# Sums, scores and a turn take other places in the inner order of a rotary attention stage

## The chip, the cores and the metric

The kernel runs on one core of one Trainium2 chip. The metric is the device time of one execution in microseconds (us). The core has TensorE (PE in the profile, its weight loads PEld), VectorE (DVE), ScalarE (ACT), GpSimd (POOL) and SyncE (SP), each with its own list of instructions that it works off in order. They meet at semaphores: an instruction may wait until a counter has a value, and may count one up when it is done.

## The reference, cut to what matters

Two layers act on x of 2 x 2048 tokens x 512. The change lies in the first, a cross attention with 128 keys per batch, 16 heads of 64, rotated queries and keys, capped scores and a causal mask:

```
q = layer_norm(query, g, b); k = layer_norm(ctx, g, b); v = layer_norm(ctx, g, b)
qh, kh = rope(heads(q @ Wq)), rope(heads(k @ Wk)); vh = heads(v @ Wv)
aw = 30 * tanh(einsum('nhtd,nhTd->nhtT', qh, kh) / sqrt(64) / 30)
p = softmax(where(pad | causal, -inf, aw))
x = x + einsum('nhtT,nhTd->nhtd', p, vh).merged @ Wo
```

Behind it come a feed-forward layer in quantised numbers, a second cross attention and a layer of eight experts. The change doesn't touch them.

## The kernel before

The first stage works in 16 chunks of 256 tokens, and a body numbered n = 0 to 16 overlaps two of them: it finishes the attention of chunk n, adds the output of chunk n-1 to x (O0 and O1, one for each 128 tokens), and prepares the queries of chunk n+1. Bodies 1 to 6 and 9 to 12 are loops on the chip, the others are written out. In each chunk the 16 heads are four units of four heads (numbers 0 to 3). For each unit:

- `project`: 48 matmuls for two units (three products of high and low parts), into a bank named Q0 to Q3; DVE rotates the result (`rotate_begin`, `rotate_end`) into `q`.
- `scores(n, b, p)`: q times keys, with 64 rows of the array for each head; ACT takes tanh and then exp (`exponentials`). On the chunks with n = 0 and n = 8 DVE multiplies a causal mask in between (`mask`).
- `sums(p)`: a matmul with 32 columns for each head adds up the probabilities over the keys; `values(n, b, p)`: probabilities times values, 64 columns for each head; ACT copies the result (`raw`).
- When all four sums are in, DVE takes their reciprocal, PE spreads it over the heads (`spread`, banks B0 to B3) and DVE multiplies (`weigh`); ACT and POOL make high and low parts of it.
- `output(t)`: 24 matmuls of 512 columns; DVE adds the bank to x (`add_out`).
- `turn_x` (X0 and X1): four transposes each of the next chunk's normalised rows; ACT scales them (`x_turned`), casts them to high parts (`x_high`), POOL makes the low parts (`x_low`), which the next projection needs.

Only two banks serve all of Q, O, X and B, in a ring whose order is Q2, Q3, O0, X0, X1, O1, Q0, Q1, B0 to B3; `begin` waits until the bank's last user has let it go. Scores have two buffers of their own, and so have the probabilities: `exponentials` of unit p waits for sums and values of unit p-2. `sums(p)` and `values(p)` wait for the exponentials of p (on masked chunks for the mask). The order of the work is written out by hand for each engine. In the code the flag `first` marks body 0, which had an order of its own.

Of the kernel before, what the change touches and what calls it, by code (L numbers as in the profile page):

```python
# [268 lines left out]
def rope_attention_stage(nc, io, xres, front_offset, ident, seen, ahead):  # L269
# [8 lines left out]
    with ExitStack() as stage:  # L278
        def sb(name, shape, dt=F32):
            return stage.enter_context(nc.sbuf_tensor("a_" + name, shape, dt))  # L280
# [58 lines left out]
        raw = xres[:, LAST_X:LAST_X + 4, 0:D]  # L339
# [78 lines left out]
        def turn_x(out, k, rows):  # L418
            for i in range(2):
                at = slice((2 * k + i) * P, (2 * k + i + 1) * P)  # L420
                for t in range(NT):
                    last = nc.tensor.transpose(out[:, i, t * P:(t + 1) * P], rows[:, t, at], ident[:])  # L422
            last.then_inc(bank_full, 1)
# [185 lines left out]
        xn = sb("xn", [P, NT, D])  # L609
# [23 lines left out]
        def of_spread(x, g):  # L633

            return x[:, g // 2, :, g % 2, :]

        with nc.Block() as block:
# [83 lines left out]
            @block.scalar  # L721
            def _(act):
                def x_turned(n, k, full, src):
                    act.wait_ge(bank_full, full)
                    for i in range(2):
                        m = 2 * k + i
                        last = nc.scalar.activation(x_full[:, m, :], src[:, i, :], ACT.Identity, bias=shift[:, m:m + 1], scale=gain[:, m:m + 1])  # L727
                    last.then_inc(freed["act"], 1)

                def x_high(k, emptied):  # L730
                    act.wait_ge(freed["act"], emptied)
                    at = slice(2 * k, 2 * k + 2)
                    nc.scalar.copy(x_hi[:, at, :], x_full[:, at, :]).then_inc(x_hi_ready, 1)  # L733

                def exponentials(n, b, p):
                    unit = n * UNITS + p
                    buf = probs[:, p % 2]
                    act.wait_ge(score_full, unit + 1)
                    if p >= 2 or not isinstance(n, int) or n >= 1:
                        act.wait_ge(pv_full, unit - 1)  # L740
                        act.wait_ge(summed, unit - 1)
                    nc.scalar.activation(buf, score_ps[:, p % 2], ACT.Tanh, scale=1.0 / (DH0 ** 0.5 * GROK)).then_inc(capped, 1)  # L742
                    act.wait_ge(capped, unit + 1)
                    nc.scalar.activation(buf, buf, ACT.Exp, bias=pad_bias[:, b:b + 1], scale=GROK).then_inc(exped, 1)

                exponentials(0, 0, 0)

                def body(n, c, b, b_next):
                    s = plan(n)

                    def use(what):
                        return ring.use(n, 0, s[what])

                    def raw(p):
                        act.wait_ge(pv_full, n * UNITS + p + 1)
                        if p % 2 == 0 and (not isinstance(n, int) or n >= 1):
                            act.wait_ge(attn_lo_ready, UNITS * (n - 1) + p + 2)
                        nc.scalar.copy(attn[:, p // 2, p % 2], pv_ps[:]).then_inc(raw_ready, 1)  # L758

                    def attn_high(g):  # L760
                        act.wait_ge(freed["dve"], use(f"B{g}").emptied[1])
                        nc.scalar.copy(of_spread(attn_hi, g), of_spread(attn, g)).then_inc(attn_hi_ready, 1)  # L762

                    first = isinstance(n, int) and n == 0
                    if "Q2" in s:
                        exponentials(n, b, 1)
                        raw(0)
                    if first:
                        exponentials(n, b, 2)
                    if "X0" in s:  # L770
                        x_turned(n + 1, 0, use("X0").full, use("X0").out)
                    if "Q2" in s and not first:
                        exponentials(n, b, 2)
                    if "Q2" in s and not first:
                        raw(1)
                        exponentials(n, b, 3)
                    if "X0" in s:
                        x_turned(n + 1, 1, use("X1").full, use("X1").out)
                        x_high(0, use("X0").emptied[1])
                        x_high(1, use("X1").emptied[1])  # L780
                    if first:
                        raw(1)
                        exponentials(n, b, 3)
                    if "Q2" in s:
                        raw(2)
                    if "X0" in s:
                        exponentials(n + 1, b_next, 0)
                    if "Q2" in s:
                        raw(3)
                        for g in range(4):  # L790
                            attn_high(g)

                chunks(act, body)
                act.wait_ge(ahead.ld_clip, 16)
                nc.scalar.activation(ahead.sigm[:], ahead.clip[:], ACT.Exp, scale=-1.0).then_inc(ahead.sig_exp, 1)
                for g in range(len(ahead.GROUPS)):
                    if g == ahead.GROUPS_AHEAD:
                        nc.scalar.activation(warm[:], minus_half[:, 0:1], ACT.Silu)
                    act.wait_ge(ahead.turned, g + 1)
                    ahead.take(nc, g, turn_places[g % len(turn_places)]).then_inc(ahead.taken, 1)  # L800
# [224 lines left out]
            def _(pe):  # L1025
# [10 lines left out]
                def place(h):  # L1036

                    return h % 2 * 2 + h // 2
# [3 lines left out]
                def scores(n, b, p):  # L1042
                    unit = n * UNITS + p
                    pe.wait_ge(q_ready, unit + 1)
                    if p >= 2 or not isinstance(n, int) or n >= 1:
                        pe.wait_ge(capped, unit - 1)
                    for h in range(4):
                        rows, m = slice(h % 2 * DH0, (h % 2 + 1) * DH0), 2 * p + h // 2
                        last = nc.tensor.matmul(score_ps[:, p % 2, place(h), :], keysT[rows, m, b * KEYS:(b + 1) * KEYS], q[rows, p % 2, h // 2, :],  # L1049
                                                start=True, stop=True)  # L1050
                    last.then_inc(score_full, 1)
# [23 lines left out]
                def body(n, c, b, b_next):  # L1075
                    s = plan(n)

                    def begin(what):
                        u = ring.use(n, 0, s[what])
                        who, count = u.reuse  # L1080
                        pe.wait_ge(freed[who], count)
                        return u.out

                    def sums(p):
                        probabilities(n, b, p)
                        if p == 0 and (not isinstance(n, int) or n >= 1):
                            pe.wait_ge(recip_ready, n)
                        for h in range(4):
                            last = nc.tensor.matmul(sum_ps[32 * h:32 * (h + 1), 0, :], sum_to[:, UNITS - 1 - p:UNITS - 1 - p + 32], probs[:, p % 2, place(h), :],
                                                    start=(p == 0), stop=(p == UNITS - 1))  # L1090
                        last.then_inc(summed, 1)
# [48 lines left out]
                    first = isinstance(n, int) and n == 0  # L1140
# [13 lines left out]
                    if "X0" in s:  # L1154
                        pe.wait_ge(xn_ready, 1 + NT * (n + 2))
                        turn_x(begin("X0"), 0, xn)
                    if first:
                        turn_x(begin("X1"), 1, xn)
                        sums(1)
                        scores(n, b, 3)  # L1160
                    elif "Q2" in s:
                        sums(0)
                        sums(1)
                        scores(n, b, 2)
                        scores(n, b, 3)
                    if "Q2" in s:
                        values(n, b, 1)
                    if first:
                        sums(2)
                    if "X0" in s and not first:  # L1170
                        turn_x(begin("X1"), 1, xn)
                    if "O0" in s:
                        output(1)
                    if "Q2" in s and not first:
                        sums(2)
                    if "Q2" in s:
                        sums(3)
                    if "X0" in s:
# [1750 lines left out]
```

## Time and profile before

| | before |
|---|---|
| three runs, us | 1512.35, 1513.0, 1513.22 |
| profiled execution, us | 1513.22 |
| its span, first to last instruction, us | 1511.4 |
| mean granted TensorE clock | 0.986 |
| PE, PEld busy, us | 1442.1, 1076.8 |
| DVE, ACT, POOL busy, us | 1183.9, 878.7, 501.7 |

The span is that of the one execution that the profiler took; its time has 1.8 us around the span. The first stage ends at some 622 us of it. In the rows a matmul's line tells what it is: L422 a turn, L430 the projection, L1032 to L1034 the output, L1049 scores, L1064 values, L1089 sums, L1103 spread. On ACT, L727 is `x_turned`, L742 tanh, L744 exp, L758 `raw`. One matmul in the code can be two instructions of the trace (f32 operands), so that the sums of one unit are eight.

### The profile page before, as it was taken

The numbers are of one execution on the slowest core, as the hardware profiler recorded it, in microseconds if no ns is written. First come the engines' busy times: TensorE is split into PE (matmuls) and PEld (weight loads), VectorE is DVE, ScalarE is ACT, GpSimd is POOL, SyncE is SP. The second block draws the span as 40 slices with busy tenths as digits, with TensorE's granted clock in tenths as the row PEclk, the third lists the DMA queues.
The fourth block names the chain that finished last, engine by engine and source line by source line (L and its number), as shares of the span: only waits on it lengthen the run. The fifth ranks groups of instructions, "written<-read, shape, count | busy, mean of one in ns | idle before, by whom it ended". The sixth has DMA issues, their size and how long they took to land. (4 is left out here: it accounts for less than half of the span.)

```text
span 1511.4 us, 30065 instructions
## 1 busy us (share of the span) xinstructions
PE 1442.1 (95%) x10610; PEld 1076.8 (71%) x10634; DVE 1183.9 (78%) x2421; ACT 878.7 (58%) x2090; POOL 501.7 (33%) x442
## 2 busy tenths in 40 slices
PE   7899999999999999899998998999999999998996
PEld 5677777777777777644443467888888877776885
DVE  6678788887887666788878967888888896786875
ACT  2444444444444443765558747888888876763442
POOL 0122222222222221200004644555555654664333
PEclk9999999999999999999999999999999999999998
DMA  8411111110111101133107610000000024225641
GB/s 300 177 46 45 45 45 45 46 41 15 37 36 45 36 8 77 46 153 154 77 1 282 240 41 3 3 2 2 4 3 3 3 86 174 114 102 180 208 148 58
DMA packets 47807, 118.34 MB, mean 78 GB/s; under 512 B 9422, under 2 KB 15950, under 8 KB 46032
## 3 DMA queue, kind: packets, MB, share of 16 engines
q1 hardware_dynamic: 42016, 100.03, 19.0%
q0 software_dynamic: 5680, 16.85, 2.8%
q8 instruction: 67, 1.10, 0.3%
q14 instruction: 44, 0.36, 0.1%
HBM read 78.90 MB, written 39.80 MB: 79 GB/s over the span
## 5 line engine op out<-in xcount | busy, mean ns | idle before, releaser
L1851 ACT ACTIVATE c_probs<-c_score,c_minus_top 128x128 f32<-128x128 f32 x512 | 183.2, 420 | 4.7 <-DVE c_minus_top L1987 4.6
L1801 POOL TENSOR_TENSOR c_probs<-c_probs,c_recip 128x1024 f32<-128x1024 f32 x64 | 121.6, 1900 | 163.1 <-DVE c_recip L1993 163.1
L700 POOL TENSOR_TENSOR a_attn_lo_parts<-a_attn,a_attn_hi_parts 128x512 fp32r<-128x512 f32 x64 | 80.6, 1294 | 201.4 <-ACT a_attn_hi_parts L762 201.4
L1851 ACT ACTIVATION_READ_ACCUMULATOR c_probs<-c_score,c_minus_top 128x1 f32 x512 | 133.3, 260 | 0.0
L758 ACT COPY a_attn<-a_pv_ps 128x512 f32<-128x512 f32 x64 | 36.6, 572 | 148.5 <-PE a_pv_ps L1064 148.5
L1478 POOL TENSOR_TENSOR xres<-xres,b_delta 128x512 f32<-128x512 f32 x24 | 48.3, 2027 | 210.6 <-DVE b_delta L1535 210.6
L430 PE MATMUL a_bank<-a_x_hi_parts,a_wq_hi 128*128 128x256 f32 x512 | 107.0, 291 | 0.3 <-PEq L445 0.3
L430 PE MATMUL a_bank<-a_x_lo_parts,a_wq_hi 128*128 128x256 f32 x512 | 103.0, 283 | 0.0
L696 POOL TENSOR_TENSOR a_x_lo_parts<-a_x_full,a_x_hi_parts 128x512 fp32r<-128x512 f32 x30 | 38.0, 1289 | 195.4 <-ACT a_x_hi_parts L733 195.4
L430 PE MATMUL a_bank<-a_x_hi_parts,a_wq_lo 128*128 128x256 f32 x512 | 102.8, 282 | 0.0
L1032 PE MATMUL a_bank<-a_wo_hi,a_attn_hi_parts 128*128 128x512 f32 x248 | 99.4, 401 | 0.0
L727 ACT ACTIVATE a_x_full<-a_bank,a_shift,a_gain 128x256 f32<-128x256 f32 x60 | 30.2, 555 | 116.9 <-PE a_bank L422 116.9
L1034 PE MATMUL a_bank<-a_wo_hi,a_attn_lo_parts 128*128 128x512 f32 x248 | 98.1, 396 | 0.0
L1033 PE MATMUL a_bank<-a_wo_lo,a_attn_hi_parts 128*128 128x512 f32 x248 | 98.0, 395 | 0.0
L2516 ACT CAST d_xT_hi<-c_score 128x512 fp32r<-128x512 f32 x67 | 39.3, 586 | 99.1 <-PE c_score L2759 92.6
L1306 ACT ACTIVATE b_silu<-b_gate,ahead_scale 128x512 f32<-128x512 f32 x88 | 60.2, 684 | 56.5 <-PE b_gate L1400 55.8
L742 ACT ACTIVATE a_probs<-a_score_ps 128x1024 f32<-128x1024 f32 x64 | 65.7, 1026 | 44.2 <-PE a_score_ps L1049 44.2
L1400 PE MATMUL b_gate<-b_xT,ahead_gateT 128*128 128x512 bf16 x339 | 87.4, 379 | 3.2 <-ACT b_xT L1283 2.7
L1341 DVE SCALAR_TENSOR_TENSOR b_hidden<-b_up,ahead_scale,b_silu 128x512 f32<-128x512 f32 x88 | 65.7, 747 | 30.7 <-PE b_up L1400 27.4
L1400 PE MATMUL b_up<-b_xT,ahead_upT 128*128 128x512 bf16 x340 | 88.9, 379 | 0.4
L430 PEld LDWEIGHTS a_bank<-a_x_hi_parts,a_wq_hi 128*128 128x128 f32 x512 | 78.9, 190 | 13.7 <-issue 6.3
L1984 DVE COPY_PREDICATED_SCALAR c_score<-c_masks,c_tiny 128x1024 f32 x64 | 82.1, 1283 | 5.2 <-issue 5.2
(358 smaller groups left out, 4304.8 us busy)
## 6 DMA issues: line engine op xcount, KB each, us to landing
hidden<-b_hidden SPq DMA_DIRECT2D x5, 2816.0 KB, 8.1
b_hidden<-hidden SPq DMA_DIRECT2D x5, 2816.0 KB, 10.6
xres<-in_x SPq DMA_DIRECT2D x8, 1024.0 KB, 14.2
d_we<-in_we SPq DMA_DIRECT2D x8, 1024.0 KB, 7.2
xres<-in_w_gate_up SPq DMA_DIRECT2D x7, 1024.0 KB, 5.4
d_got<-rows SPq DMA_DIRECT2D x20, 258.0 KB, 2.9
xres<-rows SPq DMA_DIRECT2D x19, 258.0 KB, 2.9
a_rot<-in_rot SPq DMA_DIRECT2D x16, 256.0 KB, 3.1
```

The source lines that it names most:

```text
L430: last = nc.tensor.matmul(out[:, i, :], w[:, k, cols], x[:, k, :], start=(j == 0 and i == 0), stop=(j == len(products) - 1 and i == 1))
L700: nc.gpsimd.tensor_tensor(of_spread(attn_lo, g), of_spread(attn, g), of_spread(attn_hi, g), ALU.subtract).then_inc(attn_lo_ready, 1)
L742: nc.scalar.activation(buf, score_ps[:, p % 2], ACT.Tanh, scale=1.0 / (DH0 ** 0.5 * GROK)).then_inc(capped, 1)
L1032: nc.tensor.matmul(out, hi, w_hi, start=first, stop=False)
L1033: nc.tensor.matmul(out, hi, w_lo, start=False, stop=False)
L1034: return nc.tensor.matmul(out, lo, w_hi, start=False, stop=last)
L1306: nc.scalar.activation(silu[:, u % RING, :], gate_ps[:, u % RING, :], ACT.Silu, scale=gate_scale[:, i:i + 1]).then_inc(silu_ready, 1)
L1341: nc.vector.scalar_tensor_tensor(hidden[:, n % KEPT, i, :], up_ps[:, u % RING, :], up_scale[:, i:i + 1], silu[:, u % RING, :], ALU.mult, A ...
L1400: last = nc.tensor.matmul(ps[:, u % RING, :], w[:, k, i * P:(i + 1) * P], xT[:, n % 2, k, :], start=(k == 0), stop=(k == KB - 1))
L1801: nc.gpsimd.tensor_tensor(part, part, recip[:, t % 2, heads].unsqueeze(2).to_broadcast([P, HALF, KEYS]), ALU.mult).then_inc(scaled, 1)
L1851: last = nc.scalar.activation(probs[:, t, at, :], score_ps[:, h, g, :], ACT.Exp, bias=minus_top[:, h, g:g + 1], accum_out=total[:, t, at:a ...
L1984: ch.step(nc.vector.copy_predicated(part, masks[:, j, t, :].unsqueeze(1).to_broadcast(shape), tiny[:].unsqueeze(2).to_broadcast(shape)))
```

## The change

The calls in the bodies of PE and ACT are put in another order for all chunks but chunk 0. There the branches are merged, and chunk 0 comes out as before. The instructions are the same in kind and number.

```
ACT:
-                    if "Q2" in s and not first:
-                        raw(1)
-                        exponentials(n, b, 3)
                     if "X0" in s:
                         x_turned(n + 1, 1, use("X1").full, use("X1").out)
                         x_high(0, use("X0").emptied[1])
                         x_high(1, use("X1").emptied[1])
-                    if first:
+                    if "Q2" in s:
                         raw(1)
                         exponentials(n, b, 3)
-                    if "Q2" in s:
                         raw(2)
PE:
-                    if first:
+                    if "Q2" in s and not first:
+                        sums(0)
+                        scores(n, b, 2)
+                    if "X0" in s:
                         turn_x(begin("X1"), 1, xn)
+                    if "Q2" in s:
                         sums(1)
                         scores(n, b, 3)
-                    elif "Q2" in s:
-                        sums(0)
-                        sums(1)
-                        scores(n, b, 2)
-                        scores(n, b, 3)
-                    if "Q2" in s:
                         values(n, b, 1)
-                    if first:
                         sums(2)
-                    if "X0" in s and not first:
-                        turn_x(begin("X1"), 1, xn)
                     if "O0" in s:
                         output(1)
-                    if "Q2" in s and not first:
-                        sums(2)
                     if "Q2" in s:
                         sums(3)
```

PE's list in a written-out chunk before, from the end of output(0) to the start of output(1); here x8 is two units of sums or of scores, x4 one, and the names are a_sum_ps for sums, a_score_ps for scores, a_pv_ps for values:

```order
L1034 MATMUL a_bank<-a_wo_hi,a_attn_lo_parts 128x512
L422 MATMUL a_bank<-ident,a_xn 128x128 x4
L1089 MATMUL a_sum_ps<-a_probs,a_sum_to 32x256 x8
L1049 MATMUL a_score_ps<-a_q,a_keysT 128x256 x8
L1064 MATMUL a_pv_ps<-a_probs,a_vals 64x256 x4
L422 MATMUL a_bank<-ident,a_xn 128x128 x4
L1032 MATMUL a_bank<-a_wo_hi,a_attn_hi_parts 128x512
```

The same piece of the changed kernel, whose lines are numbered four lower:

```order
L1030 MATMUL a_bank<-a_wo_hi,a_attn_lo_parts 128x512
L422 MATMUL a_bank<-ident,a_xn 128x128 x4
L1085 MATMUL a_sum_ps<-a_probs,a_sum_to 32x256 x4
L1045 MATMUL a_score_ps<-a_q,a_keysT 128x256 x4
L422 MATMUL a_bank<-ident,a_xn 128x128 x4
L1085 MATMUL a_sum_ps<-a_probs,a_sum_to 32x256 x4
L1045 MATMUL a_score_ps<-a_q,a_keysT 128x256 x4
L1060 MATMUL a_pv_ps<-a_probs,a_vals 64x256 x4
L1085 MATMUL a_sum_ps<-a_probs,a_sum_to 32x256 x4
L1028 MATMUL a_bank<-a_wo_hi,a_attn_hi_parts 128x512
```

X1's turn now stands between scores(2) and sums(1), and the sums of unit 2 stand ahead of output(1). Behind output(1) only the sums of unit 3 are left.

ACT's list in such a chunk before, from the tanh of unit 2 on:

```order
L742 ACTIVATE a_probs<-a_score_ps 128x1024
L744 ACTIVATE a_probs<-a_probs,a_pad_bias 128x1024
L758 COPY a_attn<-a_pv_ps 128x512
L742 ACTIVATE a_probs<-a_score_ps 128x1024
L744 ACTIVATE a_probs<-a_probs,a_pad_bias 128x1024
L727 ACTIVATE a_x_full<-a_bank,a_shift,a_gain 128x256 x2
L733 CAST a_x_hi_parts<-a_x_full 128x512 x2
```

And in the changed kernel:

```order
L742 ACTIVATE a_probs<-a_score_ps 128x1024
L744 ACTIVATE a_probs<-a_probs,a_pad_bias 128x1024
L727 ACTIVATE a_x_full<-a_bank,a_shift,a_gain 128x256 x2
L733 CAST a_x_hi_parts<-a_x_full 128x512 x2
L758 COPY a_attn<-a_pv_ps 128x512
L742 ACTIVATE a_probs<-a_score_ps 128x1024
L744 ACTIVATE a_probs<-a_probs,a_pad_bias 128x1024
```

X1's evacuation and the casts moved ahead of raw(1) and the exponentials of unit 3.

## Rows read from the trace of the kernel before

**Rows 1.** Windows: us, busy of each engine (instructions), granted clock, DMA share, GB/s.

```profile
94.47:552.07 457.60, 457.60 (x3330) 356.70 (x3329) 363.46 (x734) 204.37 (x286) 107.50 (x91) 1.00 0.12 40
...
552.07:587.34 35.27, 35.27 (x257) 27.29 (x255) 21.58 (x41) 15.73 (x22) 7.57 (x6) 1.00 0.17 59
```

**Rows 2.** Timeline, PE, one chunk: start us, us, engine, line, what, count.

```profile
200.06 0.60 PE L422 MATMUL a_bank<-ident,a_xn 128*128 128x128 f32 x4
200.59 1.07 PE L1089 MATMUL a_sum_ps<-a_probs,a_sum_to 128*32 128x256 f32 x16
201.59 2.00 PE L1049 MATMUL a_score_ps<-a_q,a_keysT 64*128 64x256 f32 x16
203.51 1.08 PE L1064 MATMUL a_pv_ps<-a_probs,a_vals 128*64 128x256 f32 x8
204.53 0.66 PE L422 MATMUL a_bank<-ident,a_xn 128*128 128x128 f32 x4
204.94 0.48 PE L1032 MATMUL a_bank<-a_wo_hi,a_attn_hi_parts 128*128 128x512 f32 x1
205.26 0.39 PE L1033 MATMUL a_bank<-a_wo_lo,a_attn_hi_parts 128*128 128x512 f32 x1
```

**Rows 3.** Timeline, PE, the same chunk behind output(1).

```profile
210.72 1.07 PE L1089 MATMUL a_sum_ps<-a_probs,a_sum_to 128*32 128x256 f32 x16
211.73 0.50 PE L430 MATMUL a_bank<-a_x_hi_parts,a_wq_hi 128*128 128x256 f32 x2
...
217.61 1.08 PE L1064 MATMUL a_pv_ps<-a_probs,a_vals 128*64 128x256 f32 x8
```

**Rows 4.** Timeline, PE, chunk 0; in brackets idle before and its releaser.

```profile
59.25 1.14 PE L1049 MATMUL a_score_ps<-a_q,a_keysT 64*128 64x256 f32 x8
60.32 1.09 PE L422 MATMUL a_bank<-ident,a_xn 128*128 128x128 f32 x8
62.31 0.64 PE L1089 MATMUL a_sum_ps<-a_probs,a_sum_to 128*32 128x256 f32 x8 [0.91 <-DVE a_probs L848]
62.88 1.13 PE L1049 MATMUL a_score_ps<-a_q,a_keysT 64*128 64x256 f32 x8
63.95 1.08 PE L1064 MATMUL a_pv_ps<-a_probs,a_vals 128*64 128x256 f32 x8
64.96 0.64 PE L1089 MATMUL a_sum_ps<-a_probs,a_sum_to 128*32 128x256 f32 x8
68.86 0.64 PE L1089 MATMUL a_sum_ps<-a_probs,a_sum_to 128*32 128x256 f32 x8 [3.25 <-DVE a_probs L848]
69.42 0.50 PE L430 MATMUL a_bank<-a_x_hi_parts,a_wq_hi 128*128 128x256 f32 x2
```

**Rows 5.** Timeline, ACT, chunk 0: tanh and exp of unit 2.

```profile
60.43 1.03 ACT L742 ACTIVATE a_probs<-a_score_ps 128x1024 f32<-128x1024 f32 x1 [3.00 <-PE a_score_ps L1049]
61.49 1.15 ACT L744 ACTIVATE a_probs<-a_probs,a_pad_bias 128x1024 f32<-128x1024 f32 x1
```

**Rows 6.** Timeline, DVE, the chunk of rows 2: add_out(1) and the reciprocal.

```profile
210.94 0.69 DVE L870 TENSOR_TENSOR xres<-a_bank,xres 128x512 f32 x1 [3.11 <-PE a_bank L1034]
211.85 1.76 DVE L973 RECIPROCAL a_swapped<-a_sum_ps 128x256 f32<-128x256 f32 x1 [0.23 <-PE a_sum_ps L1089]
```

**Rows 7.** Timeline, DVE and PE, the same chunk: weigh and spread(1).

```profile
220.76 1.28 DVE L931 TENSOR_TENSOR a_attn<-a_bank,a_attn 128x512 f32<-128x512 f32 x2
...
222.31 0.61 PE L1103 MATMUL a_bank<-a_recip,a_pick_heads 128*128 128x256 bf16 x4
...
223.05 1.29 DVE L931 TENSOR_TENSOR a_attn<-a_bank,a_attn 128x512 f32<-128x512 f32 x2 [1.01 <-PE a_bank L1103]
```

**Rows 8.** Waits, 94.47 to 587.34 us: total us, times, longest us.

```profile
PEld a_bank L430 <- issue: 4.2, 10, 0.4
...
PEld a_bank L430 <- POOL a_x_lo_parts L696: 1.6, 4, 0.4
```

**Rows 9.** Windows, columns as in rows 1: the first stretch at the lower clock.

```profile
70.20:73.60 3.40, 3.40 (x18) 3.40 (x17) 2.67 (x5) 0.00 (x0) 0.00 (x0) 0.50 0.00 0
```

## The prediction

> **What bounds the kernel now.** I read the page's busy shares and slices first, and they only say that TensorE (PE) is the engine to look at. The windows by stage say more. From 94.47 to 552.07 us, thirteen chunks of the first stage, PE's matmuls cover 457.60 of 457.60 us at a granted clock of 1.00, which is the 2.4 GHz level; VectorE (DVE), ScalarE (ACT) and GpSimd (POOL) are busy 363, 204 and 108 us of it, and the next chunk reads the same way [rows 1]. So in this stretch nothing that another engine does is late for PE by a visible amount: time is what PE needs for its own list. The ends of matmuls are modelled, so I trust the distances from one start to the next more than "busy", and I read those in the timeline of one chunk [rows 2, 3]. One chunk takes 457.60 / 13 = 35.20 us.
>
> In the part that the edit touches the starts are: X0 turned at 200.06, the sums of units 0 and 1 at 200.59, their neighbours, the scores of units 2 and 3, at 201.59, values(1) at 203.51, X1 turned at 204.53, output(1) at 204.94 [rows 2], and behind output(1) the sums of units 2 and 3 at 210.72 and the next projection at 211.73 [rows 3]. The reader is to see that the pieces of one kind stand together: both sums in 1.00 us, both scores in 1.92 us, both later sums in 1.01 us.
>
> Chunk 0 already runs nearly the new list, because the code has a branch for it. It is the price list for this change: sums of one unit before scores 0.57 us (62.31 to 62.88), scores of one unit before a turn 1.07 us (59.25 to 60.32), before values 1.07 us (62.88 to 63.95), values before sums 1.01 us (63.95 to 64.96), sums of one unit before a projection 0.56 us (68.86 to 69.42) [rows 4].
>
> **The change part by part.** It adds no instruction and takes none away. On PE it cuts the pair of sums, the pair of scores and the second pair of sums in two, and moves X1's turn between scores(2) and sums(1), and sums(2) ahead of output(1). On ACT it puts X1's evacuation and both casts of x ahead of raw(1) and the exponentials of unit 3. There are no DMAs in the moved steps, and none of the SP or POOL queue's own instructions change place; the two bank-ring turns X0, X1 and then O1 keep their order, so each bank still goes to the same next user. Since PE is full, the cost is the sum of PE's distances before and after:
>
> - before: 200.06 to 204.94 is 4.88 us, and 210.72 to 211.73 is 1.01 us, together 5.89 us [rows 2, 3];
> - after: X0 0.53 (it stands before sums, as now), sums(0) 0.57, scores(2) 1.07, X1 0.53 (it now stands before sums as X0 does; before output it took 204.53 to 204.94, 0.41), sums(1) 0.57, scores(3) 1.07, values(1) 1.01, sums(2) 0.57, sums(3) 0.56: together 6.48 us [rows 2, 4].
>
> That is +0.59 us a chunk: 0.14 for the first sums, 0.22 for the scores, 0.12 for the second sums, 0.12 for X1's new neighbour (0.60 by rounded parts). Chunks 1 to 14 have all of it: 14 x 0.59 = 8.3 us. Chunk 15 has no X0 and X1: before 1.00 + 1.92 + 1.02 + 1.01 = 4.95 us, after 0.57 + 1.07 + 0.57 + 1.07 + 1.01 + 0.57 + 0.56 = 5.42 us, +0.47 us. Chunks 0 and 16 keep their list. Sum: +8.7 us.
>
> The trace has no row for a turn that stands between scores and sums. Its nearest rows are 0.53 (turn before sums) and 0.41 (turn before output) [rows 2]; I take 0.53, as what follows seems to set it. With 0.41 the sum is 8.7 - 14 x 0.12 = 7.0 us. Upwards, the largest addition seen at a change of kind is the 0.22 of the scores; once more in each of 14 chunks it would make 11.8 us. These are the ends of the unknown cost.
>
> On this a page speaks. The trace shows a fixed cost each time PE goes from 128-row, 128-column matmuls to 32-column, 64-row or 64-column ones [rows 2, 4]. The Trainium skill, page "TensorEngine Tiling (Array Packing)", section "Key Properties", says that changing the tiling mode drains the array, and changing only the tile within a mode doesn't. The trace agrees in kind. The page has no price; the Trainium skill's "TensorE: Matmul & The Clock Gate", section "Step-by-step: what each phase is for", gives the drain as about 128 cycles, an estimated 0.05 us at 2.4 GHz, and with three more changes of mode in each of 15 chunks that would make an estimated 2.4 us instead of 8.7. The rows price them at 0.59 / 3 = 0.20 us each, so I don't use the page's figure.
>
> **Waits that the new order could add.** sums(2) now stands directly behind values(1), not behind 5.8 us of output(1), and waits for the exponentials of unit 2. In chunk 0 the tanh starts 1.18 us after the scores (59.25 to 60.43) and the exp ends at 61.49 + 1.15 = 62.64, 3.39 us after them [rows 4, 5]. sums(2) is due 1.07 + 0.53 + 0.57 + 1.07 + 1.01 = 4.25 us after scores(2) starts: 0.9 us to spare. In chunk 15, without X1, it is 3.72 us: 0.3 us to spare. In chunk 8 a causal mask of DVE comes in between, 0.69 us of work that starts just behind the exp, so there the step is due about when it is released; I add nothing for it, at most 0.2 us once. ACT's queue behind those exponentials gets X1 and the casts earlier and unit 3 later, but unit 3's are wanted only behind output(1).
>
> The reciprocal: DVE's chain starts when all sums are in. Now add_out(1) at 210.94 fits under the two sums and the reciprocal starts at 211.85, 0.12 us behind the projection's start at 211.73 [rows 3, 6]. With only one sum behind output(1), add_out(1) and its 0.6 us are what the reciprocal waits for: it starts about 210.94 + 0.61 = 211.55 where the projection starts at 211.28, so relative to PE it is 0.15 us later. What hangs on it: the two rotations, then weigh(0) and weigh(1), which end at 220.76 + 1.28 = 222.04 where spread(1) starts on PE at 222.31 [rows 7]. 0.27 us less 0.15 us leaves 0.12 us, about what a signal takes. I take 0, and at most 0.1 us a chunk, 1.5 us, if it falls short.
>
> What it gives: x_hi and x_lo of the next chunk are ready some 3 us earlier, as ACT does them before raw(1) and unit 3. The pause of the weight loads before the projection is put to POOL's x_lo 4 times for 1.6 us, and to nothing ("issue") 10 times for 4.2 us [rows 8]; both are 0.4 us each, so the pause is that of the changed tile and x_lo merely came last. PE's starts agree: the projection follows its sums after 1.01 us. I count 0; x_lo no longer being late is worth nothing while nothing waits for it.
>
> **The sum.** The profiled execution is one of 1513.2 us with a span of 1511.4 us; the median of the three is 1513.0 us. +8.7 us makes 1521.9 us against the profiled one and 1521.7 us against the median, which I forecast. All that follows the stage is only moved back by as much.
>
> **The rivals.**
> - Switches are cheap (7%). If a change of kind costs only what the first output matmul shows behind a turn, 0.32 us against 0.23 us for the others, 0.09 us [rows 2], three more in 15 chunks are 4.1 us: 1517 us. Against it stand the split pieces of chunk 0, which were measured at their full distance.
> - New waits (14%). DVE's chain misses spread(1) and sums(2) waits in chunks 8 and 15: + 1.5 + 0.5 us, 1523.7 us. For it speak the margins of 0.1 us; against it that the next wait in the chain (weigh(2)) has 1 us of DVE idle before it and takes up what slipped.
> - Faster (2%). If the pause before the projection really is x_lo being late, and the cuts cost nothing because the weight loads run ahead, the gain is 1.6 + 4.2 = 5.8 us: 1507 us. It decides from the point where x_lo comes later than the sums' last matmul leaves room. Against it: the same 0.4 us pause stands where no x_lo is concerned.
> - Later stages (7%). In eight stretches, the first at 70.20 us, seven more behind 620 us, the granted clock was 0.50, the 1.2 GHz level. The first came behind 3.25 us in which PE waited for a mask [rows 4, 9]. It holds 18 matmuls in 3.40 us; the projection's 48 take 5.88 us [rows 3], so 18 take 2.2 us, and the stretch costs 1.2 us. Moved by 8.7 us, the later stages could get two more or two fewer: 1524 or 1519 us.
>
> **How the numbers follow.** The forecast's own case, 1520 to 1523.5 us, has 70%. Less than 0.2%, 3.0 us, is about what a measurement of this kernel can tell from no change. The forecast, the waits, the cheap switches and the later stages are all slower by more than that: 98%, of which I move 3% to no change, for switches cheaper still. So slower 95%, no change 3%, faster 2%. The range for 8 in 10 reaches from 1518.8 us (turn between scores and sums at 0.41, one slow stretch fewer) to 1524.5 us (the waits, and one slow stretch more, or the larger price of the turn).
>
> **What the profile will show.** If I am right: a chunk of 35.8 us instead of 35.2 us, with PE's window still filled; sums of one unit at 0.57 us three or four times a chunk, scores at 1.07 us; x_lo on POOL done 3 us before its projection; DVE's reciprocal about 0.3 us behind the projection's start. If the chunk takes over 35.9 us, a wait is in it, and I look first at spread(1) and sums(2). A chunk of 35.2 us or less would prove the price list of chunk 0 wrong; a chunk of 35.8 us with another total would put the difference in the later stages.

## The result, and the profile after

| | before | after |
|---|---|---|
| median of runs, us | 1513.11 (6 runs, 1512.35 to 1516.01) | 1521.41 (6 runs, 1519.28 to 1523.35) |
| profiled execution, its span, us | 1513.22, 1511.4 | 1522.23, 1520.4 |
| mean granted clock | 0.986 | 0.986 |

The ratio of after to before is 1.0053, with a 95% interval of 1.0043 to 1.0064: slower by 0.53%. The two medians lie 8.3 us apart. The ratios, here and below, leave out one execution of the kernel before that took 2044 us at a mean clock of 0.654. The forecast was 1521.7 us in a range of 1518.8 to 1524.5 us, and slower.

The busy shares of the page after say little again:

```profile
PE 1453.4 (96%) x10634; PEld 1073.8 (71%) x10634; DVE 1204.9 (79%) x2421; ACT 880.0 (58%) x2090; POOL 505.1 (33%) x442
```

Nor does the window that in [rows 1] showed PE filled; it is as full, and only fewer instructions fit into it (3280 where 3330 did):

```profile
94.47:552.07 457.60, 457.60 (x3280) 345.84 (x3279) 376.64 (x714) 203.79 (x285) 108.36 (x89) 1.00 0.12 40
```

What answers to [rows 2, 3] is the timeline of PE in the same chunk (rows of the output and of the projection left out; the last row but one is behind output(1), the last is the next chunk's X0):

```profile
202.04 0.60 PE L422 MATMUL a_bank<-ident,a_xn 128*128 128x128 f32 x4
202.57 0.64 PE L1085 MATMUL a_sum_ps<-a_probs,a_sum_to 128*32 128x256 f32 x8
203.14 1.13 PE L1045 MATMUL a_score_ps<-a_q,a_keysT 64*128 64x256 f32 x8
204.20 0.66 PE L422 MATMUL a_bank<-ident,a_xn 128*128 128x128 f32 x4
204.79 0.64 PE L1085 MATMUL a_sum_ps<-a_probs,a_sum_to 128*32 128x256 f32 x8
205.36 1.13 PE L1045 MATMUL a_score_ps<-a_q,a_keysT 64*128 64x256 f32 x8
206.42 1.08 PE L1060 MATMUL a_pv_ps<-a_probs,a_vals 128*64 128x256 f32 x8
207.44 0.64 PE L1085 MATMUL a_sum_ps<-a_probs,a_sum_to 128*32 128x256 f32 x8
...
213.79 0.64 PE L1085 MATMUL a_sum_ps<-a_probs,a_sum_to 128*32 128x256 f32 x8
...
237.91 0.60 PE L422 MATMUL a_bank<-ident,a_xn 128*128 128x128 f32 x4
```

No row has idle time before it. The distances are those of the price list from chunk 0, 0.57 us for sums and 1.06 us for scores, but for X1's turn, which takes 0.59 us (204.20 to 204.79). The next chunk starts at 237.91: 35.87 us a chunk, where before had 35.20.

DVE's and ACT's instructions are the same in both programs, so each has its partner, and the difference of their starts shows where the time went. DVE's instructions start equally early at the first chunk (-0.03 us), then fall back by about 0.67 us with each of 14 chunks, by 0.5 us with chunk 15, and are 9.8 us late at the stage's end. Behind the stage some is given back: two partners at the end and behind the feed-forward layer are

```profile
793.27 0.74 DVE L1341 SCALAR_TENSOR_TENSOR b_hidden<-b_up,ahead_scale,b_silu 128x512 f32<-128x512 f32 x1
...
895.58 1.51 DVE L1970 TENSOR_SCALAR c_xn<-xres,c_mv,c_rstd 128x512 f32<-128x512 f32 x1 [0.66 <-POOL c_rstd L1789]
```

before, and after

```profile
803.42 0.74 DVE L1330 SCALAR_TENSOR_TENSOR b_hidden<-b_up,ahead_scale,b_silu 128x512 f32<-128x512 f32 x1
...
902.53 1.51 DVE L1959 TENSOR_SCALAR c_xn<-xres,c_mv,c_rstd 128x512 f32<-128x512 f32 x1 [0.67 <-POOL c_rstd L1778]
```

10.15 us apart, then 6.95. In between before has two stretches of PE's lower clock, 1.2 GHz. In the changed kernel the first is half as long (3.4 us for 6.8 us) and the second is not there; DVE's partners gain 1.5 us at the one and 1.7 us at the other. Windows before (the granted clock is the number behind the five busy times and their counts in brackets), then after:

```profile
797.30:804.10 6.80, 6.05 (x15) 2.20 (x16) 6.16 (x11) 6.80 (x5) 0.00 (x0) 0.50 0.00 0
882.60:886.00 3.40, 3.40 (x10) 2.66 (x9) 2.65 (x7) 1.34 (x2) 0.56 (x1) 0.50 1.03 395
```

```profile
807.70:811.10 3.40, 2.90 (x7) 1.04 (x8) 2.84 (x7) 3.40 (x4) 0.00 (x0) 0.51 0.00 0
811.10:814.50 3.40, 3.40 (x17) 1.57 (x16) 3.32 (x5) 3.40 (x2) 0.00 (x0) 0.99 0.00 0
892.30:895.70 3.40, 3.40 (x18) 2.99 (x17) 2.69 (x5) 1.20 (x3) 0.56 (x1) 1.00 0.78 281
```

Further on it is the other way round: the changed kernel is slow for 6.8 us from 1377.8 us on, where before has 3.4 us, and for 3.4 us once more at 1401.8 us (granted clock 0.50 and 0.52). It loses 2 us again, 1.6 us of them there, and at the end it is 9.0 us later.

### The profile page after: what moved, and what is told of

Its sections match the earlier page's. It is cut to its first block and busy times, and to the rows that moved or that the text cites. A ratio compares the mean times of both kernels' runs of the same rounds, so it can differ in the third digit from the quotient of the medians.

```text
span 1520.4 us, 30089 instructions
## 1 busy us (share of the span) xinstructions
PE 1453.4 (96%) x10634; PEld 1073.8 (71%) x10634; DVE 1204.9 (79%) x2421; ACT 880.0 (58%) x2090; POOL 505.1 (33%) x442
## 5 line engine op out<-in xcount | busy, mean ns | idle before, releaser
L696 POOL TENSOR_TENSOR a_x_lo_parts<-a_x_full,a_x_hi_parts 128x512 fp32r<-128x512 f32 x30 | 41.1, 1391 | 153.2 <-ACT a_x_hi_parts L733 153.2
```

## The experiments

My theory was that the whole loss is TensorE's: each time it goes from one tile shape (rows x columns of the array that a matmul takes) to another, there is a fixed cost, and cutting pairs adds changes. Rivals were a cost of ACT's new order, a cost of the waits that each unit begins with, a cost of any change of operands, a plain drain of 0.05 us, and a loss that belongs to the later start.

All compare with runs of the kernel before on the same chip. "Stage" is how much later than before the stage ends less how much later its first chunk starts, by the partners of DVE's instructions in the profiled executions; since the prologue before it differs by up to 2 us from execution to execution, this is the sharper number.

| run | chunk, us | stage, us | ratio of times (95%) |
|---|---|---|---|
| the change | 35.87 | +9.8 | 1.0053 (1.0043 to 1.0064) |
| act_only | 35.19 | -0.1 | 1.0003 (0.9991 to 1.0014) |
| pe_only | 35.91 | +10.4 | 1.0078 (1.0062 to 1.0093) |
| split_first | 35.55 | +5.2 | 1.0027 (1.0017 to 1.0037) |
| sum2_early | 35.84 | +10.4 | 1.0070 (1.0052 to 1.0087) |
| x1_between | 35.77 | +7.7 | 1.0041 (1.0026 to 1.0057) |
| values_cut | 35.71 | +7.0 | 1.0049 (1.0032 to 1.0065) |
| extra_waits | 35.20 | +0.0 | 0.9998 (0.9981 to 1.0015) |
| same_tile_cut | 35.19 | +0.1 | 1.0004 (0.9992 to 1.0016) |
| x1_kept | 35.67 | +7.6 | 1.0048 (1.0031 to 1.0065) |
| shift_only | 35.20 | +0.0 | 1.0053 (1.0035 to 1.0071) |

**act_only.** ACT's part of the diff alone.

```
                     if "X0" in s:
                         x_turned(n + 1, 1, ...); x_high(0, ...); x_high(1, ...)
-                    (raw(1) and exponentials(n, b, 3) ahead of this, but for chunk 0)
+                    if "Q2" in s:
+                        raw(1); exponentials(n, b, 3); raw(2)
```

> Only ACT's part of the change: X1's evacuation and the casts ahead of raw(1) and the exponentials of unit 3; PE keeps its list of before. My theory (the cost is PE's changes of tile shape): a chunk stays at 35.20 us, at most 0.01 us less since x_lo comes 2 to 3 us earlier, and the total stays within 1 us of 1513. Rival (the cost or a part of it comes from ACT's order, because unit 3's exponentials come late): a chunk grows by some of the 0.67 us that the changed kernel has more, the total by 2 to 9 us. Second rival (x_lo was late before): a chunk falls by 0.1 us or more, the total by over 1.5 us.

Measured: 35.19 us a chunk and no difference in the total. POOL's x_lo is done at 206.09 + 3.14 = 209.23, and the projection starts at 210.97:

```profile
206.09 3.14 POOL L696 TENSOR_TENSOR a_x_lo_parts<-a_x_full,a_x_hi_parts 128x512 fp32r<-128x512 f32 x2 [11.16 <-ACT a_x_hi_parts L733]
```

The loss is not ACT's, and x_lo was not late before, or so little (0.01 us a chunk) that it doesn't tell.

**pe_only.** PE's part of the diff alone, ACT as before.

> Only PE's part of the change; ACT keeps its order of before. My theory: a chunk takes 35.87 us as in the changed kernel, the stage ends 9.8 us later than before, the total is 8 to 10 us above before. Rival (PE's list needs ACT's new order, and either alone behaves otherwise): x_lo now comes relatively earlier to PE by only 0.5 us and a wait before the projection remains, so that the chunk takes more than 35.95 us; or, if the cost were ACT's, a chunk of 35.2 us.

Measured: stage +10.4 us, more than the whole change. In the same chunk the last sums start 0.63 us ahead of the projection, not 0.57, and POOL's x_lo ends at 211.60 + 2.55 = 214.15, just ahead of the projection at 214.28:

```profile
211.60 2.55 POOL L696 TENSOR_TENSOR a_x_lo_parts<-a_x_full,a_x_hi_parts 128x512 fp32r<-128x512 f32 x2 [14.09 <-ACT a_x_hi_parts L733]
```

So the loss is PE's, and my expectation (35.87 us exactly) missed 0.04 us, a wait for x_lo. ACT's timeline shows where it comes from:

```profile
207.41 0.58 ACT L758 COPY a_attn<-a_pv_ps 128x512 f32<-128x512 f32 x1 [1.03 <-PE a_pv_ps L1064]
```

With PE's new list values(1) starts 4.38 us behind X0's turn (201.90 to 206.28), where it was 3.45 us. ACT's raw(1) waits 1.03 us for it, and in ACT's old order unit 3's exponentials and X1's evacuation stand behind raw(1). ACT's new order takes this wait away; that is what it is worth in the change, 0.5 us.

**split_first.** Only the first sums and the scores are cut.

```
-                        sums(0); sums(1); scores(n, b, 2); scores(n, b, 3)
+                        sums(0); scores(n, b, 2); sums(1); scores(n, b, 3)
```

> PE's order: sums(0), scores(2), sums(1), scores(3), values(1), then X1, output(1), sums(2), sums(3) as before. ACT as before. My theory: a cut costs its two changes of shape, 0.14 us for the sums (2 x 0.57 against 1.00) and 0.20 us for the scores (2 x 1.065 against 1.93), 0.34 us a chunk: 35.54 us, 15 chunks, total +5.1 us. Rival (the cost comes with the waits that each unit has, or is that of X1's place): less than 0.1 us a chunk. Rival (a change costs only an array drain of some 0.05 us): 0.1 us a chunk, +1.5 us.

Measured: 35.55 us and +5.2 us, as forecast. The drain of 0.05 us would have given +1.5 us, and falls.

**sum2_early.** Only sums(2) moved, ahead of X1 and output(1).

```
                         values(n, b, 1)
+                        sums(2)
                     (X1, output(1))
-                        sums(2)
                         sums(3)
```

> PE's order of before, but sums(2) behind values(1) and ahead of X1 and output(1). ACT as before. My theory: the pair of sums is cut, 2 x 0.57 against 1.00, +0.13 us a chunk: 35.33 us, total +2.0 us. If sums(2) waited for the exponentials of unit 2 the PE's starts would show a gap before it, and the cost would be over 0.2 us a chunk; I expect no gap (0.3 us or more to spare, as scores(2) is followed by scores(3) and values(1) only, 0.86 + 1.01 us, against some 3.4 us for tanh and exp: here I expect a gap of up to 0.6 us after all, since X1's turn and the second sums no longer lie between; then the chunk takes up to 35.9 us).

Measured: 35.84 us and +10.4 us, the second of the two that I had named. The timeline shows the gap, 205.15 to 206.66 where values takes 1.01 us:

```profile
205.15 1.08 PE L1064 MATMUL a_pv_ps<-a_probs,a_vals 128*64 128x256 f32 x8
206.66 0.64 PE L1089 MATMUL a_sum_ps<-a_probs,a_sum_to 128*32 128x256 f32 x8 [0.43 <-ACT a_probs L744]
207.24 0.66 PE L422 MATMUL a_bank<-ident,a_xn 128*128 128x128 f32 x4
```

0.50 us of a chunk's 0.64 us are a wait for unit 2's exp, and 0.14 us the cut. This run is a mirror of the change: sums(2) may go ahead of output(1) only since something stands between scores(2) and it.

**x1_between.** Only the scores are cut, by X1's turn.

```
                         scores(n, b, 2)
+                        turn_x(begin("X1"), 1, xn)
                         scores(n, b, 3)
                         values(n, b, 1)
-                    (X1's turn)
```

> PE's order of before, but X1's turn between scores(2) and scores(3); the sums are not cut. ACT as before. My theory: scores cut (2 x 1.065 against 1.93, +0.20), the turn gets a 64-row neighbour on both sides: 0.58 to 0.60 against 0.41, +0.18, and output(1) behind values +0.02: +0.40 us in 14 chunks, 35.59 us, total +5.6 us. Rival (a switch costs the same whatever stands beside it, 0.20 us a change): two more changes, +0.40 us too; so it is the split of the sum that tells: a turn of 0.41 us here would put the price on scores alone. Rival (drain of 0.05 us): +0.1 us.

Measured: the pieces came out as expected, scores 1.07 us, turn 0.58 us, scores 1.07 us:

```profile
203.07 1.13 PE L1049 MATMUL a_score_ps<-a_q,a_keysT 64*128 64x256 f32 x8
204.14 0.66 PE L422 MATMUL a_bank<-ident,a_xn 128*128 128x128 f32 x4
204.72 1.13 PE L1049 MATMUL a_score_ps<-a_q,a_keysT 64*128 64x256 f32 x8
205.79 1.08 PE L1064 MATMUL a_pv_ps<-a_probs,a_vals 128*64 128x256 f32 x8
...
212.59 1.07 PE L1089 MATMUL a_sum_ps<-a_probs,a_sum_to 128*32 128x256 f32 x16
213.78 0.50 PE L430 MATMUL a_bank<-a_x_hi_parts,a_wq_hi 128*128 128x256 f32 x2
```

The total was 2 us more, because the last two rows are 1.19 us apart and not 1.01: the wait for x_lo again, 0.18 us a chunk, with ACT's old order. I had not counted it. A turn between two shapes costs 0.17 us more than beside the output.

**values_cut.** values(1) in two halves with X1's turn between them.

```
-                        values(n, b, 1)
+                        values(n, b, 1, range(2))      (heads 0 and 1)
+                        turn_x(begin("X1"), 1, xn)
+                        values(n, b, 1, range(2, 4))   (heads 2 and 3)
```

> The kernel before, but values(1) cut in two halves of two heads, with X1's turn between them: two more changes of tile shape in 14 chunks, no unit cut, no wait moved. My theory: each half takes 0.43 + 0.15 = 0.58 us, the turn 0.58 us, together 1.75 us against 1.43 us before, +0.33 us a chunk: 35.52 us, total +4.7 us. Rival (the price lies in a unit's start, in its waits or its semaphore signal): the halves have only one of each, so at most 0.1 us a chunk.

Measured: 0.59, 0.58 and 0.59 us, 1.76 us where 1.75 was expected:

```profile
206.70 0.65 PE L1065 MATMUL a_pv_ps<-a_probs,a_vals 128*64 128x256 f32 x4
207.29 0.66 PE L422 MATMUL a_bank<-ident,a_xn 128*128 128x128 f32 x4
207.87 0.65 PE L1065 MATMUL a_pv_ps<-a_probs,a_vals 128*64 128x256 f32 x4
208.46 0.50 PE L1032 MATMUL a_bank<-a_wo_hi,a_attn_hi_parts 128*128 128x512 f32 x1
```

Here too the wait for x_lo adds some 0.17 us a chunk, which is the rest of +7.0 us. The price stands inside one unit, with one set of waits and one signal, so it doesn't belong to a unit's beginning or end.

**extra_waits.** Three more waits, long fulfilled, in every unit's sums and scores.

```
                     for h in range(4):
+                        if h >= 1:
+                            pe.wait_ge(q_ready, unit + 1)
                     (and in sums)
                         for h in range(4):
+                            if h >= 1:
+                                probabilities(n, b, p)     (a wait for exp or the mask)
```

> The kernel before with three more waits in each unit's sums and scores, each for a semaphore that has long been reached; no instruction of PE's changes its place. My theory (the price is that of a changed tile shape): the chunk stays at 35.20 us, sums of two units at 1.00 us and scores of two at 1.93 us, total within 1 us of before. Rival (a piece costs more because it begins with waits): each wait costs 0.02 us or more, 24 of them a chunk 0.5 us or more, 35.7 us.

Measured: nothing. Sums of two units take 1.00 us, scores of two 1.92 us:

```profile
202.77 1.07 PE L1093 MATMUL a_sum_ps<-a_probs,a_sum_to 128*32 128x256 f32 x16
203.77 2.00 PE L1051 MATMUL a_score_ps<-a_q,a_keysT 64*128 64x256 f32 x16
205.69 1.08 PE L1066 MATMUL a_pv_ps<-a_probs,a_vals 128*64 128x256 f32 x8
```

**same_tile_cut.** X1's turn cut in two around the first three matmuls of output(1), all with 128 rows and 128 columns; ACT in the new order.

```
-                        turn_x(begin("X1"), 1, xn)
-                        output(1)
+                        turn_x(x1, 1, xn, (0,))
+                        output(1, lambda: turn_x(x1, 1, xn, (1,)))   (called behind k == 0)
```

> ACT's part of the change, with PE's order of before in which X1's four turns are cut in two: two turns, the first three matmuls of output(1), two turns, the rest of output(1). Both kinds use all 128 rows and 128 columns. My theory (the price is that of a changed tile shape): the cut costs under 0.1 us a chunk, 35.2 to 35.3 us, total at most +1.5 us. Rival (any change from one kind of matmul to another costs 0.15 us or more, because the banks and operands change): two more changes, 0.3 us or more a chunk, 35.5 us, total +4 us or more.

Measured: nothing. From the first turn to the sums are 6.185 us, as in the kernel before, to 0.01 us:

```profile
204.18 0.44 PE L422 MATMUL a_bank<-ident,a_xn 128*128 128x128 f32 x2
204.38 0.48 PE L1029 MATMUL a_bank<-a_wo_hi,a_attn_hi_parts 128*128 128x512 f32 x1
204.69 0.40 PE L1030 MATMUL a_bank<-a_wo_lo,a_attn_hi_parts 128*128 128x512 f32 x1
204.93 0.39 PE L1031 MATMUL a_bank<-a_wo_hi,a_attn_lo_parts 128*128 128x512 f32 x1
205.16 0.38 PE L422 MATMUL a_bank<-ident,a_xn 128*128 128x128 f32 x2
205.30 0.48 PE L1029 MATMUL a_bank<-a_wo_hi,a_attn_hi_parts 128*128 128x512 f32 x1
```

With values_cut this is the pair that decides: mixed with matmuls of the same tile shape, the four turns cost nothing more; set between matmuls of another shape, they cost 0.33 us more. It was tried with turns and output matmuls alone.

**x1_kept.** The changed kernel with X1's turn left beside output(1).

```
                         values(n, b, 1)
                         sums(2)
+                    (X1's turn, not between scores(2) and sums(1))
                     output(1)
```

> The changed kernel, but with X1's turn left next to output(1): sums(0), scores(2), sums(1), scores(3), values(1), sums(2), X1, output(1), sums(3). ACT as in the changed kernel. My theory (prices of neighbours add up): the cuts of the first sums and scores 0.34 us, the cut of the second sums 0.15 us with what it does to its neighbours, nothing for X1, as a turn beside output costs 0.41 us: a chunk of 35.70 us where the changed kernel has 35.87 us, stage +7.5 us, total +6 to +8 us. sums(2) is due 3.71 us after scores(2) starts and its exponentials end after 3.4 us: no gap, but in chunk 8 with its mask about 0.4 us. Rival (X1's place between scores(2) and sums(1) is needed to cover the exponentials): a gap before sums(2) of 0.1 us or more in every chunk, 35.8 us or more.

Measured: 35.67 us a chunk and +7.6 us; the prices add up. In chunk 8 there is the wait for the mask, 0.45 us. X1's place costs 0.20 us of the change's 0.67.

**shift_only.** 82 projection matmuls more in the prologue, all else only moved back.

```
+                extra = begin_first(PRE_Q + 1)
+                (3 x 24 and once 10 matmuls into extra)
                 project(extra, 1)
```

> The kernel before with 82 more projection matmuls ahead of the second projection of the prologue; their result is overwritten. All behind it is only moved back, by 82 x 0.119 = 9.8 us, as the changed kernel's later stages were. My theory: chunks of 35.20 us, the stage ends 9.8 us later (less what the prologue hides), and the later stages move by the same amount but for their slow stretches, which fall elsewhere: the total comes out between 7.5 and 11 us above before, and single runs differ by over 1 us with the number of slow stretches. Rival (the later stages run a fixed 0.8 us faster when they start later): total +9.0 us in all runs. Rival (the loss in the chunks is the later start's, not the order's): the chunk grows.

Measured: chunks of 35.20 us, the first of them 11.6 us later (the 9.8 us and a longer slow stretch in the prologue), the stage's end 11.6 us later, the program's end 6.9 us later in the profiled execution. The later stages lost slow time at the same two places as with the change, half of the stretch at the first (808.8 us) and all of it at the second (894 us):

```profile
808.80:815.60 6.80, 5.93 (x22) 2.50 (x23) 6.13 (x12) 6.80 (x5) 0.00 (x0) 0.75 0.00 0
894.00:897.40 3.40, 3.40 (x17) 2.94 (x16) 2.76 (x3) 0.95 (x2) 0.56 (x1) 1.00 0.69 239
```

From the stage's end to 900 us the two gave back 3.4 us. Single runs go from 1517.9 to 1523.7 us. So the later stages can give time back though no order is changed. But the later start doesn't decide it. In pe_only, where the stage ends 10.0 us later than before, both stretches are whole:

```profile
806.90:813.70 6.80, 5.76 (x14) 2.09 (x15) 6.13 (x12) 6.80 (x5) 0.00 (x0) 0.50 0.00 0
892.20:895.60 3.40, 3.40 (x9) 2.72 (x9) 2.62 (x7) 1.48 (x1) 0.56 (x1) 0.50 1.00 373
```

So they are in sum2_early, also 10.0 us later, while split_first, only 4.3 us later, has lost the same half and the same whole as the change (granted clock 0.75 and 1.00). Why a stretch falls or not at a place stays open: I have windows of single executions, no cause. The scatter of the times goes with the mean clock: of 16 runs of the changed kernel the five with 0.988 or 0.989 take 1519.3 to 1520.5 us, the eleven with 0.985 to 0.987 take 1521.8 to 1523.4 us.

## Why the prediction was right

**The bound.** PE was filled before and is filled after, and the loss is in its list alone: pe_only has it, act_only doesn't.

**The cuts.** The price list of chunk 0, sums, scores and values, held to 0.01 us. The cuts of the first sums and of the scores were forecast at 0.36 us a chunk by rounded parts, 0.34 in the expectations, and split_first shows 0.35. The cut of the second sums was 0.12 and is 0.12 to 0.14 (sum2_early, x1_kept).

**X1's turn.** This is the term that was mis-sized. I took 0.53 us, that of a turn which comes from the same tile shape and goes to another, as if only what follows set it. Coming from scores it takes 0.59 us. The row for it stood in [rows 2]: the turn behind values is 0.66 us long there, the turn behind output 0.60 us, for the same four instructions. With 0.06 us more, and 0.01 to 0.02 us in output(1), which now stands behind sums, the 0.59 us become the measured 0.67 us, and the 8.7 us of the sum the stage's 9.8 us.

**What was counted at nothing.** sums(2) is not late in any chunk, not even in chunk 8: each stands 1.02 us behind values(1). The 0.9 us and the 0.3 us to spare are borne out: sum2_early, whose sums(2) come 2.94 us behind scores(2), waits 0.50 us, which puts its release at 3.44 us, and x1_kept, due at 3.71 us, doesn't wait but in chunk 8. The reciprocal was forecast at 0.15 us later against PE; DVE's chain now starts at 214.62 where the projection starts at 214.36, 0.26 us behind it where it was 0.12, so 0.14 us. The spread at 224.96 stands 1.07 us behind its scores, as before, and the weigh ahead of it ends at 223.51 + 1.28 = 224.79, so it waits for nothing:

```profile
214.01 0.69 DVE L866 TENSOR_TENSOR xres<-a_bank,xres 128x512 f32 x1 [2.18 <-PE a_bank L1030]
214.62 1.75 DVE L969 RECIPROCAL a_swapped<-a_sum_ps 128x256 f32<-128x256 f32 x1
...
223.51 1.28 DVE L927 TENSOR_TENSOR a_attn<-a_bank,a_attn 128x512 f32<-128x512 f32 x2
```

x_lo is ready 3.5 us ahead of the projection (208.02 + 2.80 = 210.82 on POOL, 214.36 on PE) and worth nothing beside the old PE list, as forecast. What I had missed is that beside the new PE list the old ACT order would have made it late; the change moved both, so the sum was not hurt.

**The later stages.** I had them move back as one. They gave back 0.8 us in the profiled execution, within the two stretches that the rival allowed; a stretch of 3.4 us cost some 1.6 us there, where the rival had 1.2 us. That is chance as far as these runs show: in pe_only the two stretches stayed. So two errors of about a microsecond each, one in the stage and one behind it, cancelled in the total; the total is closer than the working deserves. The upper end of the range was also loosely added: the waits and a slow stretch make 1523.7 + 1.2 = 1524.9 us, and the larger price of the turn 1524.8 us, where it says 1524.5 us.

**The count of changes.** The prediction counts three more changes of tile shape a chunk and so 0.20 us for each. From X0's turn to the projection the two lists have six and ten: four more in chunks 1 to 14, and three more in chunk 15, which has no turn. By its own 0.59 us a change costs 0.15 us; measured, the stage's 9.8 us over 59 changes are 0.17 us each, as in split_first (0.35 us for two) and values_cut (0.33 us for two). The forecast didn't use the count, but the rival of cheap switches did: at 0.09 us it would have been 5.3 us and not 4.1.

**The drain.** The rule of the Trainium skill ("TensorEngine Tiling (Array Packing)", section "Key Properties") that a change of mode drains the array and a change of tile within the mode doesn't fits all runs in kind. The estimate of 0.05 us a change, from the 128 cycles that the Trainium skill's "TensorE: Matmul & The Clock Gate" gives for a drain (section "Step-by-step: what each phase is for"), was about a third of what a change cost here; over 59 changes it makes an estimated 3.1 us, not 9.8. What makes up the rest, the first weights of the next shape coming late or something else, no run separates.

No version beat the kernel before. Its list already groups what has one shape; X1's turn stands where it takes 0.41 us, and no place tried has less, and the only piece of the change that costs nothing, ACT's order, gains nothing either beside the old PE list.

## What to carry to other kernels

Where TensorE is filled from end to end, read its timeline by distances of starts and look for a chunk, a prologue or a tail that already runs the new order: it is a price list, and it was right to 0.01 us here for every piece that it held. A piece that it doesn't hold needs a row with the same neighbours on both sides. Keep matmuls of one tile shape together; a unit set apart from its like costs 0.14 to 0.20 us, an insertion of the same shape nothing, a wait that is long fulfilled nothing. When an order on a filled engine is changed for the sake of a wait, first show that the engine waits.

## What the runs showed of the hardware that I had not expected

- The cost of a change of tile shape lies on both sides of it: four turns take 0.41 us between values and output, 0.53 us between output and sums, 0.59 us between scores and sums. Cutting the turns by output matmuls, which have the same shape, costs under 0.01 us (6.185 us with the cut and without).
- Waits on semaphores that have long been reached cost PE nothing: with 24 more of them a chunk takes 35.20 us, as without.
- Later stages which do the same work gave back 4.7 us in one execution (shift_only), 3.4 us of it at two places where a slow stretch was shorter or gone, and 0.1 us there in another execution that came to them almost as late (pe_only, 10.0 us). The kernel before alone takes 1508 to 1516 us from execution to execution. Differences of 0.5% between single executions can be this alone; the stage's own length is the number to compare.
